# First phase of a two-layer decoder kernel: taps of the convolution that read the accumulation bank, C·B at the end of its chain, and the steps in another order

## The reference, cut to what matters

```python
x = x + _L0_attn_ref(_layernorm(x), ...)             # chains M, V, N
x = x + _L0_xattn_ref(_layernorm(x), ctx, ctx, ...)  # chains Y, X
x = x + _L0_ffn_ref(_layernorm(x), ...)              # chain F: shared expert, router, scatter
# in _L0_attn_ref:
proj = einsum('btd,pd->btp', x, in_proj_w)           # x_ssm 512, z 512, B 128, C 128, dt 32
xc = conv over 4 steps, one filter per channel, + conv_b
x_ssm = silu(xc);  dt = softplus(dt_in + dt_bias);  A_bar = exp(-exp(A_log) * dt)
h_t = A_bar h_{t-1} + dt B_t x_t;  y_t = C_t h_t + D x_t
y = rmsnorm(y) * silu(z);  return y @ out_proj_w
```

## Time and profile before

| | |
|---|---|
| median of 3 runs | 4827.91 us (4826.06 to 4829.62) |
| profiled execution | 4827.89 us, of it span 4826.3 |
| PE busy | 4224.3 us (88%) |
| DVE busy | 3368.1 us (70%) |
| ACT busy | 2909.1 us (60%) |
| POOL busy | 2734.9 us (57%) |
| granted clock of PE, whole span | 0.923 |

### The profile page before, as it was taken

One profiled execution on the slowest core, in us unless ns is written; L12 is line 12 of the kernel. 1 busy time (PEld: TensorE's weight loads), 2 busy tenths in 40 slices (PEclk: granted clock), 3 DMA queues, 4 the chain that ended last, 5 costly groups with the idle time before them and its releaser, 6 DMA issues.

```text
span 4826.3 us, 119218 instructions
## 1 busy us (share of the span) xinstructions
PE 4224.3 (88%) x33430; PEld 3093.7 (64%) x33431; DVE 3368.1 (70%) x8668; ACT 2909.1 (60%) x7030; POOL 2734.9 (57%) x4093
## 2 busy tenths in 40 slices
PE   3788888888888888888869979999999999999998
PEld 2666666666666666666647756666666666666665
DVE  2776677666776667766745547777777777777776
ACT  2666666666666666666634436666666666666564
POOL 3666666666666666666622235555555555555554
PEclk9888888888888888888979989999999999999998
DMA  5222222222222222222214411111111111111110
GB/s 155 72 82 90 74 74 74 89 83 74 74 78 92 75 74 74 83 88 75 74 59 145 144 39 31 30 31 31 31 29 31 30 31 31 31 31 31 31 31 18
DMA packets 215885, 304.09 MB, mean 63 GB/s; under 512 B 56608, under 2 KB 167456, under 8 KB 215840
## 3 DMA queue, kind: packets, MB, share of 16 engines
q1 hardware_dynamic: 188864, 240.33, 16.0%
q0 software_dynamic: 19200, 52.45, 3.3%
q10 hardware_dynamic: 7776, 10.75, 0.7%
HBM read 239.19 MB, written 64.23 MB: 63 GB/s over the span
## 4 chain that ended last, share of the span: by engine, by line
PE 51%; POOL 20%; issue 17%; DVE 6%; ACT 2%; POOLq 1%; SPq 1%; DMA 0%; DVEq 0%; ACTq 0%
PE Q L1397 14%; PE Q L1402 8%; POOL arena L618 7%; PE Q L1390 6%; PE Q L1488 4%; PE Q L1425 3%; PE Q L1735 3%; PE Q L1768 3%; PE Q L1589 3%; PE Q L1434 2%; POOL arena L625 2%; PE Q L1601 2%; POOL arena L605 1%; PE Q L1419 1%; POOL arena L606 1%
## 5 line engine op out<-in xcount | busy, mean ns | idle before, releaser
L1402 PE MATMUL Q<-ident,arena 128*128 128x128 f32 x4768 | 801.5, 291 | 148.7 <-ACT arena L1145 35.3
L1402 PEld LDWEIGHTS Q<-ident,arena 128*128 128x128 f32 x4768 | 557.0, 145 | 388.2 <-issue 123.7
L1397 PE MATMUL Q<-Wkvl,arena 128*128 128x512 f32 x1024 | 500.3, 601 | 0.0
L618 POOL TENSOR_TENSOR arena<-arena 128x1024 f32<-128x1024 f32 x256 | 479.4, 1889 | 7.2 <-DMA arena<-cum_rows 7.2
L682 POOL TENSOR_TENSOR l<-l,half_pow 128x8 f32<-128x8 f32 x192 | 318.5, 1659 | 233.2 <-DVE l L1025 231.3
L707 POOL TENSOR_TENSOR arena<-arena,part_of 128x512 f32<-128x512 f32 x256 | 263.7, 1041 | 190.8 <-DVE part_of L1063 190.4
L1488 PE MATMUL Q<-arena 128*16 128x128 f32 x4096 | 223.6, 339 | 169.1 <-DVE arena L847 167.9
L769 DVE TENSOR_REDUCE mx<-Q 128x4 f32<-128x512 f32 x512 | 343.9, 681 | 10.2 <-PE Q L1419 5.5
L1425 PEld LDWEIGHTS Q<-ident,arena 128*128 128x128 f32 x2048 | 244.2, 148 | 116.5 <-issue 84.9
L1425 PE MATMUL Q<-ident,arena 128*128 128x128 f32 x2048 | 314.0, 288 | 1.3 <-ACT arena L1155 0.4
L1155 ACT ACTIVATE arena<-Q,mx 128x128 f32<-128x128 f32 x1024 | 281.8, 372 | 0.7 <-DVE mx L769 0.5
(11 more groups left out here) (310 smaller groups left out, 10753.3 us busy)
## 6 DMA issues: line engine op xcount, KB each, us to landing
arena<-cum_rows SPq DMA_DIRECT2D x256, 512.0 KB, 6.1
arena<-routed_rows SPq DMA_DIRECT2D x144, 128.0 KB, 2.1
expert_rows<-arena POOLq DMA_DIRECT2D x144, 128.0 KB, 2.0
arena<-in_x_dram SPq DMA_DIRECT2D x128, 128.0 KB, 4.4
arena<-in_ctx_dram SPq DMA_DIRECT2D x128, 128.0 KB
x_rows<-arena SPq DMA_DIRECT2D x128, 128.0 KB, 1.7
arena<-x_rows SPq DMA_DIRECT2D x128, 128.0 KB, 2.3
out_dram<-arena SPq DMA_DIRECT2D x64, 128.0 KB, 1.7
```

The lines of the kernel that those rows point to most:

```text
L618: tell(g.tensor_tensor(E8[j], E8[j], cums[:, 8 * j:8 * j + 8].unsqueeze(2).broadcast_to([P, 8, T]), ALU.subtract), "diff")
L1397: last = mm(out, lhs(c), rhs(c), start=c == 0, stop=c == n - 1)
L1402: last = nc.tensor.transpose(out[:, c * P:(c + 1) * P], src[:, c * P:(c + 1) * P], ident[:, :])
```

## The change

The first phase alone is changed. ACT's copy of the projection and the tile `xpad` are gone; the taps read Q[1] directly. The tap that is `late` steps late writes the columns from `late` on, so no zero columns are needed; the first tap covers all columns and is now an instruction with two scalar columns (`tensor_scalar`) in place of one with a spread tile. `cb` (and PE's `CB`) go behind `gz` and `z`; so bc of the next sequence waits for `cbm` in place of `gz`, and N's first masked product waits for `cbm`. And the five lists of `ORDER[1]` are others.

```diff
@@ ORDER[1], two of five lists @@
         "POOL": """
-            Nd0 Nd1 Nd2 Xx1r Fln3 Xln2 Mln1 Nd3 Msp Nm3 Fsc Nyg Nrms
+            Nd0 Nd1 Nd2 Nd3 Xx1r Fln3 Mln1 Xln2 Fsc Msp Nm3 Nyg Nrms
         """,
         "SP": """
-            Ncb0 Ncb1 Ncb2 Yc Xm Mx Ncb3 Nx Mco Fm Fo
+            Ncb0 Xm Ncb1 Ncb2 Yc Ncb3 Mx Fm Nx Mco Fo
@@ DVE, chain V @@
-                yield "cv"
-                done(dve, "xpad", b)
-                for k in range(NCONV):
-                    if k:
-                        yield f"cv{k}"
+                for late in range(NCONV):
+                    yield f"cv{late}"
+                    if late == 0:
+                        done(dve, "ip1", b)
                     for c in range(IC):
-                        src, wk = xpad[:, c, k:k + T], convw[:, c, k:k + 1]
-                        out = xc[:, c * T:(c + 1) * T]
-                        if k == 0:
-                            last = v.scalar_tensor_tensor(out, src, wk, convb[:, c:c + 1].broadcast_to([P, T]), ALU.mult, ALU.add)
+                        src, wk = Q[1][:, c * T:(c + 1) * T - late], convw[:, c, NCONV - 1 - late:NCONV - late]
+                        out = xc[:, c * T + late:(c + 1) * T]
+                        if late == 0:
+                            last = v.tensor_scalar(out, src, wk, convb[:, c:c + 1], ALU.mult, ALU.add)
                         else:
                             last = v.scalar_tensor_tensor(out, src, wk, out, ALU.mult, ALU.add)
...
-                yield "cb"
-                done(dve, "CB", b)
-                was(dve, "M3", b)
-                tell(v.tensor_tensor(cbm, Q[1][:, 0:T], triu[:, :], ALU.mult), "cbm")
...
                 tell(v.scalar_tensor_tensor(gz, tz, 1.0, Q[1][:, :], ALU.add, ALU.mult), "gz")
+                yield "cb"
+                done(dve, "CB", b)
+                was(dve, "M3", b)
+                tell(v.tensor_tensor(cbm, Q[1][:, 0:T], triu[:, :], ALU.mult), "cbm")
@@ DVE, chain N @@
                 for j in range(3):
                     yield f"m{j}"
+                    if j == 0:
+                        done(dve, "cbm", b)
@@ ACT, chain V @@
-                yield "xp"
-                done(act, "ip1", b)
-                tell(s_.activation(xpad[:, :, NCONV - 1:], cut(Q[1][:, :], IC), ACT.Copy), "xpad")
@@ PE, chain V @@
                 yield "bc"
                 done(pe, "ln1_T", b)
-                was(pe, "gz", b)
+                was(pe, "cbm", b)
...
-                yield "CB"
-                done(pe, "xpad", b)
-                tell(mm(Q[1][:, 0:T], bcT[:, 0, :], bcT[:, 1, :], start=True, stop=True), "CB")
                 yield "xsT"
                 done(pe, "xs2", b)
-                done(pe, "cbm", b)
...
+                yield "CB"
+                done(pe, "gz", b)
+                tell(mm(Q[1][:, 0:T], bcT[:, 0, :], bcT[:, 1, :], start=True, stop=True), "CB")
```

20 lines of the change are left out of this document (9 added, 11 removed).

## The result

The changed kernel takes 4911.02 us, median of 4 runs (4908.52 to 4921.0), beside 4826.99 for the kernel before in the same session: ratio 1.018, 95% interval 1.0162 to 1.0198. The forecast was 4756. All of the difference lies in the first phase: it ends some 80 us later, and phases two and three are as long as they were.

What follows compares the result with a forecast made beforehand. A loop of waits was taken to bound the first phase, with DVE's 14.8 us without a pause at its heart. Ten terms gave 36.1, plus 0.2 for hops 36.3 us per body for 37.5, 72 us less: 4756 us, range 4708 to 4838.

Steps and rivals of the forecast that it cites:

- The stretch without a pause: On DVE, M0 to M2 and two maxima leave it; ratio to end of taps takes 8.1 us for 14.1.
- E: Softplus on POOL, L594 to the start of L622: 7.55 us less the hold-ups of L605 and L606, 5.9.
- The taps: Convolution on DVE: sixteen taps reading Q[1] at 0.34 us each, 4.5 us with hops against 6.8 before.
- POOL's d0 to d3 follow yg and rms and end well ahead of the next x2: POOL's four differences, 4 x 1.89 us, end well before the next x2; their transfers go out in the same window.
- Term J: Body's end on DVE: 0.3 to x1, then start of L861 to end of L880 1.8, together 2.1 us.
- Term D: Scatter on POOL, now ahead of the softplus: two of 1.10 and issue pauses of together 0.45, 2.65 us.
- Term F: M3 on POOL: 1.89 us as L618, 1.95 with a hop, not held up beside taps that read Q.
- Term C: Router, L889 to the end of L912: 5.6 less the 0.91 wait, less 0.1, plus 0.2, 4.8 us.
- G and H: G: fourth block, copy, turns, a block of scores and its mask, 4.1 us; H: Xm2 and xdt, 2.1 us.
- The quicker rival: PE's low-clock stretch behind its wait goes too, turns and Wr 0.6 us shorter: 35.7 per body, 4720 us; chance 0.20.
- The convolution's path takes over: Two of slower taps (+2.2), ln1 held on POOL (+1.2), low-clock ip1 (+1.9) keep the body at 37.5: 4828 us; chance 0.12.
- The slower rival: DVE's M products hold up POOL's norm instructions (+0.65) and scatter (+1.2): 38.15 us per body, 4867 us; chance 0.14.

Runs made afterwards that it cites:

- xm_only: Changed kernel with one token of SP's list moved, the mask's transfer (Xm) behind Yc as before: 4848.05 us, ratio 1.0046.
- xm_fillall: Changed kernel with Xm behind Yc, plus unread extra products in each of PE's waits ahead of x's projection: 4893.69 us, ratio 1.0143.
- xm_copy: Changed kernel with Xm behind Yc, but ACT's copy of the projection and the old taps from SBUF: 5067.08 us, ratio 1.0499.
- sp_old: Changed kernel with SP's old order (Xm behind Yc, Ncb3 behind Mx, Mco ahead of Fm): 4844.68 us, ratio 1.0033.
- taps_alone: Taps out of Q[1], no copy, C·B at the chain's end, lists otherwise those of the kernel before: 4826.95 us, ratio 0.9994.
- before_fill: Kernel before with five unread extra products on PE ahead of N's first block: 4824.4 us, ratio 0.9989.
- taps_fill_d2: Taps out of Q[1], old order, five unread products ahead of N's first block, POOL's third difference moved behind the norms: 4822.28 us.
- taps_wv: Taps out of Q[1], old order, no extra products, Wv's product moved ahead of N's first block: 4827.93 us, ratio 1.0003.

## Why the prediction was wrong, step by step

*The stretch without a pause, right for POOL, half right for DVE.* M0 to M2 and two maxima left it, but DVE has no pause from the first tap to y0. The softplus follows the scatter without a pause, and L603 and L604 are free of L847: E came out at 5.84 for 5.9. C·B at the chain's end cost nothing, as forecast: bc waits for ACT's copy (0.55), not for the mask.

*The taps, right in size.* Sixteen in 1.37 + 2.27 + 1.10 = 4.7 us with the joins, forecast 4.5; no wait beside M3. The first tap is 405 ns long, the others 341, and 256 and 768 rows hardly vary:

```profile
L815 DVE TENSOR_SCALAR arena<-Q,convw,convb x256: 399/405/414, 62.6 to 2494.8; 128x128 f32<-128x128 f32 x128
```

```profile
L817 DVE SCALAR_TENSOR_TENSOR arena<-Q,convw,arena x768: 334/341/351, 64.0 to 2499.7; 128x127 f32<-128x127 f32 x64, 128x126 f32<-128x126 f32 x64, 128x125 f32<-128x125 f32 x64
```

The quicker end (0.28) and the slower (0.48) were both off. The Trainium skill's prices (VectorE: DVE Perf Modes, The TRN2 errata) would have made them an estimated 1.0 us longer than SBUF taps; the rows say 0.2 to 0.3, all of it in the four `tensor_scalar`.

*"POOL's d0 to d3 follow yg and rms and end well ahead of the next x2; their transfers go out in the same window", wrong.* This is the largest step that an experiment prices: 63 us of the 84 by which the kernel is slower, and of the 155 between forecast and result. I looked at SP's list only for who waits there, not for how long the transfers take to land after the softplus, though the differences read them. In the kernel before, three differences had little room already; they end 0.20 us before x2 starts at 1045.03:

```profile
1039.24 5.59 POOL L618 TENSOR_TENSOR arena<-arena 128x1024 f32<-128x1024 f32 x3
```

Now there are four, 7.5 us of work, and 9.9 us from the end of rms (1033.16) to the next x2 (1043.10). That would have done. But yg came sooner, so POOL met transfers that had not landed, with two waits of 1.45 and 1.47 us, and 10.4 us are too much. The transfers themselves are hardly slower than they were, 6.5 us from issue to landing at the median of the phase for 6.1 before; with Xm behind them it is 5.5. d3 then ran into x2. Term J became 2.98 for 1.8 in the body shown. xm_only shows it: 4848 for 4911. It doesn't explain the sign alone, since xm_only is still 0.46% slower than the kernel before (0.29% to 0.62%). Note that x2's hold-up is the same one that I had read off for taps and M3, and I did not ask which other DVE sums of two SBUF inputs the new order puts beside a POOL difference.

*Term D, the scatter, 3.53 for 2.65.* The row of the scatter starts 0.82 us after the slots end, and the first takes 1.43 beside the third masked product. Before, it stood in a pause, where neither showed; the 1.10 of the earlier trace rows was the mean of a first scatter of 1.23 us and a second of 0.96.

*Term F, "beside taps that read Q it isn't held up", wrong.* M3 (L620) takes 2.35 in all 64 bodies, and as much with no tap beside it (xm_fillall: it starts while DVE is at scores); beside taps from SBUF it takes 2.40 (xm_copy). So of the 2.41 of the earlier trace rows some 0.05 was a hold-up and the rest its own length, and L618 was the wrong row to size it by.

*Term C, 5.5 for 4.8.* The rank waits for bc at the low clock (0.92 before L908) and the router's row for ACT (0.52).

*G and H were 5.5 for 6.2, I 7.8 for 7.5, B 1.9 for 1.8, A 3.5 as forecast.* All terms together 38.96 for 36.1, 1.2 of it J. C, D, F and I were sized 2.3 us too short together, G and H 0.7 too long. At this price alone the gain of 1.2 per body was gone, and xm_only (37.5 in most bodies) has nothing left of it. So two steps failed, one path that was put at nothing (the transfers and x2, 1.2 us in the body shown, 63 us) and terms on the loop that were too small, C, D and F above all.

*The quicker rival, wrong way round.* The low stretch did not go, it grew and took the projection with it: Wv, Wq, the scores and the gate, which had stood ahead of the projection, now stand ahead of PE's wait or behind the projection, and between L847 and the projection PE has short products with waits between them.

*"The convolution's path takes over", nearest of the rivals.* It wanted two of three, and two came: ip1 at the low clock (3.62 for 1.95, +1.7) and ln1 held on POOL (L583 1.04 for 0.19, +0.85), with taps at their forecast rate. That is 2.5 of the 2.6 us to spare (the sums of the prediction give 2.8). In sp_old, xm_only and the changed kernel DVE takes y0 without a wait behind xs2 in most bodies, and the first two have bodies of 37.5, as the rival had it. It did not have the 1.2 us at x2. xm_fillall frees this path (DVE waits 2.37 us for PE ahead of xs2) and is no faster, because POOL's sum is as long.

*The slower rival* had the right kind of mechanism at the wrong place. L583 of ln1 takes 1.04 and the first scatter 1.43, some 1.2 together of the 1.85 that it counted; and the decisive meeting was of x2 with a difference. The Trainium skill (SBUF — State Buffer, Who interferes with whom) says that a Vector instruction with two SBUF inputs contends with a GpSimd instruction that reads SBUF. L880 beside L616, 1.65 for 0.43, agrees, and so does L897, 1.04 and 1.10 for 0.235; by that sentence both were candidates that I could have named. Its other half, that issuing descriptors needs the write side, would leave the scatter free, and the first scatter speaks against it: 1.43 beside a product with two SBUF inputs, 1.12 in taps_alone.

*What was not in the forecast at all:* that neither DVE's shorter stretch nor a higher clock of PE brings anything alone (taps_alone, before_fill), and both together do. Two paths of nearly the same length in the body before would explain it; this is argued from the four runs, not seen in one trace.

*What stays open.* Bodies of 37.5 us came up in the kernel before, before_fill, taps_alone, taps_fill_d2, taps_wv, sp_old and xm_only, with quite different work in them; the rows show that the time saved returned as products at half clock, not why at this length. So the 21 us that xm_only is still behind can't be put on one term.
